# First head's maxima and shift made in the projection stage of an attention and expert kernel

## The chip, the cores and the metric

The kernel runs on one core of a Trainium2 chip. TensorE (PE) multiplies matrices; PEld is its weight load. VectorE (DVE), ScalarE (ACT) and GpSimd (POOL) work on tiles in SBUF and PSUM; SyncE (SP) issues most of the DMAs. Each engine takes its own instructions in the order in which they were written and waits at semaphores for the others. The metric is the device time of one execution in microseconds (us), the median of several runs.

## The reference, cut to what matters

```python
def reference(x, Wq, bq, Wk, bk, Wv, bv, Wo, bo, wg, bg, w1, b1, w2, b2, gamma, beta):
    xn = _layernorm(x)                      # x: 4 x 2048 x 256
    # attention, 16 heads of 16
    q, k, v = (heads(xn @ W.T + b) for W, b in ((Wq, bq), (Wk, bk), (Wv, bv)))
    probs = softmax(einsum('bqhd,bkhd->bhqk', q * 0.25, k))
    att = einsum('bhqk,bkhd->bqhd', probs, v).reshape(b, s, d) @ Wo.T + bo
    # experts: every token keeps 2 of 16, every expert takes 1024 of 2048 tokens of a batch
    scores = softmax(xn @ wg + bg)
    masked = scores * one_hot(top_k(scores, 2)).sum(-2)
    route = masked / (masked.sum(0) + 1e-6) * 4
    _, seq_ids = top_k(transpose(route), 1024)
    ...
    return x + att + layernorm(xn + scattered_expert_outputs) * gamma + beta
```

## The kernel before

Four stages run one after the other, each in a block of its own; at the end of a block all engines wait for each other.

- `norm`: layernorm of 16 blocks of 512 tokens, the transposed tokens into `tok_all`, v into `v_all`, the router's `logits`.
- `project`: q and k of all heads. A chunk is one half (128 features) of q or k for one block of 512 tokens: two matmuls into `qk_ps[m]` (L385), m = 0 to 3 over q's and k's halves, so 64 chunks. ACT takes each chunk out of PSUM twice: in full precision into `f32s[m]` (L409) and rounded into `parts[m]` (L411). POOL puts the rest that the rounding left beside it (L424), and SP stores both parts to `q_parts` and `k_parts` in DRAM (L432), 512 KB a chunk. PE may write `qk_ps[m]` again when ACT has rounded the chunk four before, and ACT may round when the store of the chunk four before has landed. So PE is at most eight chunks ahead of the stores that have landed. Beside this DVE makes the routing weights, a chain of small operations (L447 to L482). After a quarter of the blocks (16 chunks) PE waits for them (`routed`), transposes them into `route_ps` (L394), four PSUM banks, and DVE copies them to `route` (L484).
- `attend`: 64 heads (16 for each of 4 batches). A head's scores are computed twice. The first pass (`pass1`, L771) takes one part of 48 rows of `q_feat` and `k_feat` to `m_ps`, a piece of 128 queries by 1024 keys in two matmuls, 32 pieces a head; DVE takes the maximum of every piece (L852). From the maxima comes the head's `shift`: `row_max` (L854), rounded on ACT (L731), split on POOL (L579), turned on DVE (L843), put into two rows of `q_feat` by four DMAs (L653). The second pass (`score`, L781) uses the upper 50 rows with the shift in them; ACT takes exp (L724) and `weigh` (L790) multiplies with v. `q_feat` and `k_feat` have two buffers each, filled by `feed` (L641 to L647) with four DMAs: a pair of parts of q, k's first part twice, and one single part of each, 768 KB in all, once for the lower rows (first pass) and once for the upper ones (second pass). In the steady steps the first pass of the next heads runs between the scores of this one. Ahead of the first step all 32 pieces of head 0 and `EARLY` = 10 pieces of head 1 run alone (L820 to L825).
- `finish`: experts, output projection, final layernorm and sum.

The steps in SP's order at the start of `attend` are: feed head 0 and head 1 low, load two bias rows, feed head 0 up (after ACT has written ones into the last 32 rows of `k_feat`, L718), feed head 2 low, put the shift.

## Time and profile before

| | us |
|---|---|
| median of 3 runs | 3444.11 (3443.16 to 3446.69) |
| the profiled execution | 3444.21 |
| its span, first to last instruction | 3442.4 |
| `norm`, from the start to PE's first chunk | 102.2 |
| `project`, to the first instruction of `attend` on POOL | 102.2 to 239.2 |
| start of `attend`, to PE's first score of head 0 | 239.2 to 315.8 |
| from that score to the end | 315.8 to 3442.4 |

Over the whole span PE is busy for 96%, DVE for 84%, ACT for 73%, POOL for 27%. The stages differ much, so the busy shares have to be read by stage. In the rows further down a line like "150.38 3.60 PE L385 MATMUL ... x8" is a start, a duration in us, engine, line and operation, and the count of records; two chunks leave eight records, since each of their four matmuls leaves two. In square brackets stands the idle time before and what ended it.

### The profile page before, as it was taken

To read this page: it belongs to the slowest core of one execution; us is meant where nothing else is said; L and a number is where in the kernel's file an instruction comes from. 1 tells how busy PE (TensorE), PEld (TensorE's weight loads), DVE (VectorE), ACT (ScalarE), POOL (GpSimd) and SP (SyncE) were. 2 spreads that over 40 slices of the span, in tenths; PEclk is the share of its full clock that TensorE was granted. 3 is DMA by queue.
4 is the path that set the end of the run, shared out by engine and by line. 5 is a ranking of instruction groups with operands and counts; after the bars stand their busy time and mean duration, and the time that the engine had idled before them with its cause. 6 is when DMAs were issued, how large, how long until landed. Compare 5 with 4: busy or idle time off the path is not lost. (4 is left out here: it accounts for less than half of the span.)

```text
span 3442.4 us, 74610 instructions
## 1 busy us (share of the span) xinstructions
PE 3296.2 (96%) x20848; PEld 1706.4 (50%) x20848; DVE 2894.2 (84%) x2987; ACT 2526.4 (73%) x5726; POOL 929.1 (27%) x1339
## 2 busy tenths in 40 slices
PE   7868999999999999999999999999999999599998
PEld 6424444444444444444444444444444444288887
DVE  7508999999999999999999999999999998267777
ACT  3452888888888888888888888888888888443433
POOL 2550222222222222222222222222222222144443
PEclk9986999999999999999999999999999999799999
DMA  6581111122111211111121111211111121355553
GB/s 198 173 241 33 50 54 54 54 60 59 58 56 55 56 56 55 54 54 54 54 60 56 56 55 54 63 56 56 55 54 54 54 59 47 112 136 169 160 164 117
DMA packets 133063, 272.29 MB, mean 79 GB/s; under 512 B 22512, under 2 KB 68656, under 8 KB 120432
## 3 DMA queue, kind: packets, MB, share of 16 engines
q1 hardware_dynamic: 130464, 266.68, 26.7%
q8 instruction: 176, 2.88, 0.4%
q10 hardware_dynamic: 2256, 1.36, 0.2%
q14 instruction: 167, 1.37, 0.1%
HBM read 173.59 MB, written 84.93 MB: 75 GB/s over the span
## 5 line engine op out<-in xcount | busy, mean ns | idle before, releaser
L852 DVE TENSOR_REDUCE half_max<-m_ps 128x1 f32<-128x1024 f32 x2048 | 2413.4, 1220 | 324.5 <-PE m_ps L771 308.8
L724 ACT ACTIVATE prob<-s_ps 128x512 f32<-128x512 f32 (+1 forms) x5120 | 2188.3, 520 | 425.8 <-PE s_ps L781 423.2
L781 PE MATMUL s_ps<-q_feat,k_feat 50*128 50x512 f32 (+1 forms) x5120 | 1538.0, 396 | 7.5 <-issue 4.7
L771 PE MATMUL m_ps<-k_feat,q_feat 48*128 48x512 f32 x4096 | 1405.1, 448 | 55.9 <-DMA k_feat<-k_parts 28.4
L781 PEld LDWEIGHTS s_ps<-q_feat,k_feat 50*128 50x128 f32 x5120 | 796.2, 184 | 983.3 <-ACT prob L724 870.6
L790 PE MATMUL a_ps<-prob,v_head 128*32 128x512 f32 x8192 | 1091.6, 605 | 0.0
L771 PEld LDWEIGHTS m_ps<-k_feat,q_feat 48*128 48x128 f32 x4096 | 616.3, 187 | 287.5 <-DVE half_max L852 248.6
L579 POOL TENSOR_TENSOR shift<-row_max,shift 128x16 fp32r<-128x16 f32 x64 | 14.2, 222 | 1213.0 <-ACT shift L731 1213.0
L790 PEld LDWEIGHTS a_ps<-prob,v_head 128*32 128x32 f32 x8192 | 161.2, 108 | 253.7 <-issue 211.7
L1134 ACT ACTIVATE g_hi<-g 128x512 fp32r<-128x512 f32 x128 | 81.0, 632 | 243.8 <-DVE g L1172 199.8
L1297 POOL TENSOR_TENSOR g_lo<-g,g_hi 128x512 fp32r<-128x512 f32 x128 | 173.0, 1352 | 229.2 <-ACT g_hi L1134 229.2
L606 POOL TENSOR_SCALAR step_of<-route,cand 64x256 f32<-64x256 f32 x217 | 198.6, 915 | 44.5 <-POOL held L607 38.3
L573 POOL COPY v_head<-v_all 128x256 f32 (+1 forms) x64 | 25.3, 397 | 660.2 <-PE a_ps L790 660.1
L607 POOL TENSOR_TENSOR held<-held,step_of 64x256 f32<-64x256 f32 x217 | 157.6, 726 | 39.8 <-POOL step_of L606 39.8
L1172 DVE TENSOR_TENSOR g<-g,mask_bc 128x512 f32<-128x512 f32 x128 | 133.5, 1043 | 36.0 <-ACT g L1131 30.7
L1067 PE MATMUL o_ps<-w_hi,g_hi 128*128 128x256 f32 x512 | 144.6, 282 | 6.1 <-issue 3.7
L1067 PE MATMUL o_ps<-w_lo,g_hi 128*128 128x256 f32 x512 | 144.3, 282 | 0.0
L1067 PE MATMUL o_ps<-w_hi,g_lo 128*128 128x256 f32 x512 | 143.1, 280 | 0.0
L1056 PE MATMUL h_ps<-xn_hi,w_hi 128*128 128x512 f32 x256 | 105.7, 413 | 32.0 <-DMA b_rows<-b_parts 32.0
L1131 ACT ACTIVATE g<-h_ps,b_col 128x512 f32<-128x512 f32 x128 | 86.2, 674 | 25.7 <-PE h_ps L1056 25.7
L1067 PEld LDWEIGHTS o_ps<-w_hi,g_hi 128*128 128x128 f32 x512 | 96.5, 189 | 12.0 <-issue 7.1
L1056 PE MATMUL h_ps<-xn_lo,w_hi 128*128 128x512 f32 x256 | 102.1, 399 | 0.0
(132 smaller groups left out, 1904.1 us busy)
## 6 DMA issues: line engine op xcount, KB each, us to landing
q_feat<-q_parts SPq DMA_DIRECT2D x128, 256.0 KB
k_feat<-k_parts SPq DMA_DIRECT2D x128, 256.0 KB
q_parts<-parts SPq DMA_DIRECT2D x32, 512.0 KB, 4.8
k_parts<-parts SPq DMA_DIRECT2D x32, 512.0 KB, 4.8
q_feat<-q_parts SPq DMA_DIRECT2D x128, 128.0 KB
k_feat<-k_parts SPq DMA_DIRECT2D x128, 128.0 KB
att_dram<-att SPq DMA_DIRECT2D x64, 256.0 KB, 14.0
mask_bc<-mask_b SPq DMA_DIRECT2D x128, 128.0 KB, 4.4
```

The lines of the kernel that those rows point to most:

```text
L606: do(pool.tensor_scalar(step_of[:, :], t["route"][:, c * PART:(c + 1) * PART], bound, None, ALU.is_ge))
L607: do(pool.tensor_tensor(held[:, :], held[:, :], step_of[:, :], ALU.add))
L724: act.activation(prob[tile(r, kt) % R][:, cols(j)], s_ps[slot(r, kt, j) % R][:, wide(j)], ACT.Exp).then_inc(exped, 1)
L771: ins = pe.matmul(m_ps[p % 2][:, k * BLK:(k + 1) * BLK], q_feat[r % 2][LOW, qt * P:(qt + 1) * P], k_feat[r % 2][LOW, key:key + BLK], start ...
L781: pe.matmul(s_ps[slot(r, kt, j) % R][:, wide(j)], k_feat[r % 2][UP, kt * P:(kt + 1) * P], q_feat[r % 2][UP, cols(j)], start=True, stop=Tru ...
L790: ins = pe.matmul(a_ps[qb * VW:(qb + 1) * VW, :], v_head[r % R][:, kt, :], prob[tile(r, kt) % R][:, qb * BLK:(qb + 1) * BLK], start=(kt == ...
L852: dve.tensor_reduce(half_max[r][:, p // 2, p % 2:p % 2 + 1], m_ps[p % 2][:, :], AX.X, ALU.max).then_inc(maxed, 1)
L1056: ins = pe.matmul(h_ps[e % 2][:, :], w, v, start=(c == 0 and k == 0), stop=(c == KC - 1 and k == 2))
L1067: ins = pe.matmul(o_ps[k], v, w[:, e, :], start=(e == 0 and m == 0), stop=False)
L1131: act.activation(g[e % 2][:, :], h_ps[e % 2][:, :], ACT.Gelu, bias=b1_col[:, e:e + 1]).then_inc(gelu, 1)
L1172: dve.tensor_tensor(g[e % 2][:, :], g[e % 2][:, :], mask_bc[q % 2][:, e % QTR, :], ALU.mult).then_inc(gated, 1)
L1297: pool.tensor_tensor(g_lo[e % 2][:, :], g[e % 2][:, :], g_hi[e % 2][:, :].bitcast(F32), ALU.subtract).then_inc(split, 1)
```

## The change

The tiles `q_feat`, `k_feat`, `half_max`, `row_max`, `shift`, `turned` and the two `m_ps` buffers, with their semaphores, now live from the projection stage on. Room is made in SBUF by keeping the weights of v and the router in `norm`, by two buffers of `f32s` in place of four, and by doing the routing in `logits` and two `work` tiles instead of four. In PSUM the routing weights are transposed into `m_ps`.

In `project` PE runs six blocks (24 chunks) before it waits for the routing. The remaining 40 chunks are written out in 20 turns of two chunks and two or three pieces: 32 pieces of head 0 and 10 of head 1. DVE takes their maxima, and the shift of head 0 is made and put at the stage's end. SP issues three feeds between the stores. The ones in `k_feat` are written by POOL at the start of `norm`. `attend` starts with head 0's scores; SP feeds head 2 low first, then loads the biases.

```diff
@@ norm, gpsimd
             pool.sem_inc(rstd_done, 2)
+            pool.wait_ge(ident_made, 1)
+            for u in range(2):
+                pool.memset(t["k_feat"][u][96:P, :].bitcast(F32), 1.0).then_inc(cleared, 1)
+                pool.wait_ge(cleared, 3 + u)
@@ project
-    f32s = [sb(f"f32s{m}", [P, BLK]) for m in range(M)]
+    f32s = [sb(f"f32s{m}", [P, BLK]) for m in range(KC)]
...
-    work = sb("work", [P, 4, TILES, E])
-    ex, tmp, hot, hot2 = (work[:, k] for k in range(4))
+    work = sb("work", [P, 2, TILES, E])
+    ex, tmp = (work[:, k] for k in range(2))
+    hot, hot2 = lg[:, :, :], tmp
@@ project, tensor
-            chunks(0, NBLK // 4)
+            def first_pass(n, p):
+                if p == 0:
+                    pe.wait_ge(fed_low[n], 16 * LOADS)
+                pe.wait_ge(maxed, n * PAIRS + p + 1)
+                qt, half = divmod(p, 2)
+                for k in range(2):
+                    key = half * 2 * BLK + k * BLK
+                    ins = pe.matmul(m_ps[p % 2][:, k * BLK:(k + 1) * BLK], q_feat[n][low, qt * P:(qt + 1) * P],
+                                    k_feat[n][low, key:key + BLK], start=True, stop=True)
+                ins.then_inc(piece, 1)
+
+            with pe.Fori(0, BEFORE) as blk:
+                for m in range(M):
+                    chunk(blk, m)
 
             pe.wait_ge(routed, 1)
...
-            chunks(NBLK // 4, NBLK)
+            early = PAIRS + EARLY
+            turns = (NBLK - BEFORE) * M // 2
+            for blk in range(BEFORE, NBLK):
+                for m in range(M):
+                    chunk(blk, m)
+                    if m % 2 == 1:
+                        at = ((blk - BEFORE) * M + m) // 2
+                        for p in range(at * early // turns, (at + 1) * early // turns):
+                            first_pass(p // PAIRS, p % PAIRS)
@@ project, scalar
-                    act.wait_ge(split, blk * M + m + 1)
-                    act.activation(f32s[m][:, :], qk_ps[m][:, :], ACT.Identity, bias=biases[m][:, m % KC:m % KC + 1], scale=scales[m])
+                    act.wait_ge(split, blk * M + m + 1 + M - KC)
+                    act.activation(f32s[m % KC][:, :], qk_ps[m][:, :], ACT.Identity, bias=biases[m][:, m % KC:m % KC + 1], scale=scales[m])
...
+            act.wait_ge(row_maxed, 1)
+            act.activation(shift[:, 0, :], row_max[0][:, :], ACT.Copy).then_inc(shift_rounded, 1)
@@ project, gpsimd
+            pool.wait_ge(shift_rounded, 1)
+            pool.tensor_tensor(shift[:, 1, :], row_max[0][:, :], shift[:, 0, :].bitcast(F32), ALU.subtract).then_inc(shift_done, 1)
@@ project, sync
-            with sp.Fori(0, NBLK) as blk:
-                for m in range(M):
-                    sp.wait_ge(split, blk * M + m + 1 + M)
-                    store(blk, m)
+            stores(0, BPS + 1)
+            for m in range(M):
+                sp.wait_ge(stored[m], 16 * BPS + 16)
+            feed(0, LOWER, fed_low)
+            stores(BPS + 1, BPS + 3)
+            feed(1, LOWER, fed_low)
+            stores(BPS + 3, BPS + 5)
+            feed(0, UPPER, fed_up)
+            stores(BPS + 5, NBLK)
+            sp.wait_ge(shift_turned, 1)
+            rows = q_feat[0][UPPER + FEAT:UPPER + FEAT + SHIFT, :].bitcast(F32).rearrange("k (q j p) -> k q j p", j=quarters, q=ST)
+            for j in range(quarters):
+                sp.dma_start(rows[:, :, j, :], turned[j * SHIFT * ST:(j + 1) * SHIFT * ST, :]).then_inc(shift_in, 16)
@@ project, vector
-            do(dve.tensor_copy(t["route"][:, :], route_ps[:, :]))
+            for half in range(2):
+                do(dve.tensor_copy(t["route"][:, half * 2 * BLK:(half + 1) * 2 * BLK], m_ps[half][0:B * E, :]))
+            dve.sem_inc(maxed, 2)
+            for p in range(PAIRS):
+                dve.wait_ge(piece, p + 1)
+                dve.tensor_reduce(half_max[0][:, p // 2, p % 2:p % 2 + 1], m_ps[p % 2][:, :], AX.X, ALU.max).then_inc(maxed, 1)
+            dve.wait_ge(maxed, PAIRS + 2)
+            dve.tensor_reduce(row_max[0][:, :], half_max[0][:, :, :], AX.X, ALU.max, negate=True).then_inc(row_maxed, 1)
+            for p in range(EARLY):
...
+            dve.wait_ge(shift_done, 1)
+            dve.transpose(turned[:, :], shift[:, :, :].rearrange("p k q -> p (k q)").bitcast(F32)).then_inc(shift_turned, 1)
@@ attend, sync
-            for n in range(2):
-                feed(n, n, LOWER, fed_low)
+            sp.wait_ge(piece, PAIRS)
+            feed(2, 0, LOWER, fed_low)
             for dst, src in ((shift_bc[:, :], "beta"), (staged[:, 0:D].bitcast(F32), "bo")):
                 sp.dma_start(dst, t[src].partition_broadcast(P)).then_inc(bias_in, 16)
-            sp.wait_ge(ones_made, 2)
-            feed(0, 0, UPPER, fed_up)
-            sp.wait_ge(piece, PAIRS)
-            feed(2, 0, LOWER, fed_low)
-            put_shift(0, 0)
@@ attend, tensor
-            for p in range(PAIRS):
-                for k in range(2):
-                    pass1(0, 0, 0, p, k)
-            for p in range(EARLY):
-                for k in range(2):
-                    pass1(1, 0, 1, p, k)
             step(0, 0, 0, first=True)
```

On PE, from the end of `project` to the first score of head 0 (`s_ps`), this is the order before:

```order
L385 MATMUL qk_ps<-tok_all,wkT_sb 128x512 x2
L380 REGISTER_ALU
L380 COMPARE_AND_BRANCH
L376 UNCONDITIONAL_BRANCH
L757 UNCONDITIONAL_BRANCH
L771 MATMUL m_ps<-k_feat,q_feat 128x512 x84
L781 MATMUL s_ps<-q_feat,k_feat 128x512
```

and this after, from the last turns of `project` on (L411 is a chunk's matmul, L423 a piece's):

```order
L411 MATMUL qk_ps<-tok_all,wqT_sb 128x512 x4
L423 MATMUL m_ps<-k_feat,q_feat 128x512 x4
L411 MATMUL qk_ps<-tok_all,wkT_sb 128x512 x4
L423 MATMUL m_ps<-k_feat,q_feat 128x512 x6
L404 UNCONDITIONAL_BRANCH
L819 UNCONDITIONAL_BRANCH
L843 MATMUL s_ps<-q_feat,k_feat 128x512
```

All 84 matmuls of pieces have moved ahead of the block's end (L404); the first score stands right behind it.

On PE behind the wait for the routing, the order after (with what each waits for); the first piece waits for head 0's feed and stands ahead of all chunks but two:

```order
L434 MATMUL m_ps<-ident,work 64x128 [waits p_routed]
L434 MATMUL m_ps<-ident,work 64x128 x15
L411 MATMUL qk_ps<-tok_all,wqT_sb 128x512 [waits p_rounded]
L411 MATMUL qk_ps<-tok_all,wqT_sb 128x512
L411 MATMUL qk_ps<-tok_all,wqT_sb 128x512 [waits p_rounded]
L411 MATMUL qk_ps<-tok_all,wqT_sb 128x512
L423 MATMUL m_ps<-k_feat,q_feat 128x512 [waits a_maxed,a_fed_low0]
L423 MATMUL m_ps<-k_feat,q_feat 128x512
L423 MATMUL m_ps<-k_feat,q_feat 128x512 [waits a_maxed]
L423 MATMUL m_ps<-k_feat,q_feat 128x512
L411 MATMUL qk_ps<-tok_all,wkT_sb 128x512 [waits p_rounded]
```

Before, the chunks behind the transposes waited for `p_rounded` alone.

On SP, from the last store of the fifth block on, the order after:

```order
L485 DMA k_parts<-parts 128x2x512 [waits p_split]
L497 REGISTER_ALU
L497 COMPARE_AND_BRANCH
L491 DMA q_feat<-q_parts 32x1x2048 [waits p_stored2,p_stored3,p_stored1,p_stored0]
L492 DMA k_feat<-k_parts 32x1x2048
L493 DMA q_feat<-q_parts 16x2048
L494 DMA k_feat<-k_parts 16x2048
L497 UNCONDITIONAL_BRANCH
L497 ISA
L485 ISA [waits p_split]
L485 DMA q_parts<-parts 128x2x512
```

The stores of the blocks that follow now stand behind the feed in SP's queue; before, the same four DMAs (L644 to L647) stood behind the end of the block.

## Rows read from the trace of the kernel before

**Rows 1.** Windows by stage: busy time and count of each engine, clock share, DMA share, GB/s.

```profile
102.00:239.00 137.00, 115.02 (x272) 51.72 (x272) 40.27 (x33) 82.59 (x129) 88.60 (x66) 0.93 0.84 245
239.00:316.00 77.00, 49.54 (x86) 21.28 (x88) 50.16 (x44) 3.92 (x3) 5.28 (x9) 0.50 0.19 49
316.00:3442.00 3126.00, 3051.42 (x20108) 1568.33 (x20108) 2729.27 (x2637) 2405.35 (x5528) 814.22 (x1225) 0.99 0.24 69
```

**Rows 2.** Timeline of PE, end of `norm` to the end of `project`.

```profile
91.48 1.04 PE L320 MATMUL xT_ps<-ident,xn 128*128 128x128 f32 x8
102.20 3.69 PE L385 MATMUL qk_ps<-tok_all,wqT_sb 128*128 x8 [1.27 <-ACTq L401]
...
142.22 3.62 PE L394 MATMUL route_ps<-ident,work 128*64 128x128 f32 x16 [12.29 <-DVE cand L482]
145.63 4.91 PE L385 MATMUL qk_ps<-tok_all,wqT_sb 128*128 x8
150.38 3.60 PE L385 MATMUL qk_ps<-tok_all,wkT_sb 128*128 x8
153.82 3.60 PE L385 MATMUL qk_ps<-tok_all,wqT_sb 128*128 x8
...
225.92 3.60 PE L385 MATMUL qk_ps<-tok_all,wkT_sb 128*128 x8
```

**Rows 3.** Timeline of PE, DVE, ACT and POOL, start of `attend`.

```profile
239.24 1.80 POOL L566 MEMSET prob<- 32x2048 f32 x1 [4.29 <-POOLq L376]
257.87 2.07 PE L771 MATMUL m_ps<-k_feat,q_feat 48*128 48x512 f32 x4 [28.35 <-DMA k_feat<-k_parts]
262.94 2.35 PE L771 MATMUL m_ps<-k_feat,q_feat 48*128 48x512 f32 x4 [0.18 <-DVE half_max L852]
264.19 2.36 DVE L852 TENSOR_REDUCE half_max<-m_ps 128x1 f32<-128x1024 f32 x2 [0.17 <-PE m_ps L771]
315.78 0.76 PE L781 MATMUL s_ps<-q_feat,k_feat 50*128 50x512 f32 x1 [4.75 <-issue]
```

**Rows 4.** Timeline of SP: pairs of stores, then the first DMA of a feed.

```profile
108.38 2.41 SPq L432 DMA_DIRECT2D q_parts<-parts  x2
134.72 2.58 SPq L432 DMA_DIRECT2D k_parts<-parts  x2
232.20 3.15 SPq L432 DMA_DIRECT2D k_parts<-parts  x2
298.25 0.65 SPq L644 DMA_DIRECT2D q_feat<-q_parts  x1
```

**Rows 5.** Windows of one us behind the feed issued at 298.25, columns as in rows 1.

```profile
303.00:304.00 1.00, 0.91 (x3) 0.47 (x2) 1.00 (x2) 0.00 (x0) 0.00 (x0) 0.50 0.14 57
310.00:311.00 1.00, 1.00 (x2) 0.32 (x2) 1.00 (x1) 0.00 (x0) 0.00 (x0) 0.50 0.14 57
312.00:313.00 1.00, 0.00 (x0) 0.00 (x0) 0.30 (x1) 0.00 (x0) 0.00 (x0) 0.50 0.83 131
```

**Rows 6.** Windows in `project`, columns as in rows 1.

```profile
180.00:230.00 50.00, 49.52 (x116) 21.66 (x114) 0.00 (x0) 36.06 (x57) 36.15 (x29) 1.00 0.99 295
```

**Rows 7.** Timeline: POOL in `norm`, splits on POOL, a routing operation on DVE, PE in a steady step.

```profile
8.35 0.22 POOL L287 TENSOR_SCALAR var<-mv 128x4 f32<-128x4 f32 x1 [6.77 <-DVE mv L230]
121.45 15.45 POOL L424 TENSOR_TENSOR parts<-f32s,parts 128x512 fp32r<-128x512 f32 x8 [0.26 <-ACT parts L411]
153.65 1.27 POOL L424 TENSOR_TENSOR parts<-f32s,parts 128x512 fp32r<-128x512 f32 x1 [0.45 <-ACT parts L411]
135.81 1.37 DVE L474 TENSOR_TENSOR denom<-work 128x256 f32<-128x256 f32 x1
346.52 1.06 PE L790 MATMUL a_ps<-prob,v_head 128*32 128x512 f32 x8
347.51 0.38 PE L781 MATMUL s_ps<-q_feat,k_feat 50*128 50x256 f32 x1
349.07 1.06 PE L790 MATMUL a_ps<-prob,v_head 128*32 128x512 f32 x8
```

More of the change, by code:

```diff
@@ L58 @@
 PART = 256
+HEAD_RING = 3
+PAIRS = ST * 2
+EARLY = 10
+LOADS = 4
+BEFORE = 6
 HALVES = NBLK * KC
@@ L133, in build @@
             cand = sb("cand", [B * E, 1], I32, ctx=first)
+            q_feat = [sb(f"q_feat{r}", [P, S], F32R, ctx=first) for r in range(2)]
+            k_feat = [sb(f"k_feat{r}", [P, S], F32R, ctx=first) for r in range(2)]
+            half_max = [sb(f"half_max{r}", [P, ST, 2], ctx=first) for r in range(HEAD_RING)]
+            row_max = [sb(f"row_max{r}", [P, ST], ctx=first) for r in range(HEAD_RING)]
+            shift = sb("shift", [P, SHIFT, ST], F32R, ctx=first)
+            turned = sb("turned", [P, SHIFT * ST], ctx=first)
+            fed_low = [sem(f"a_fed_low{r}") for r in range(2)]
+            fed_up = [sem(f"a_fed_up{r}") for r in range(2)]
+            piece, maxed, row_maxed = sem("a_piece"), sem("a_maxed"), sem("a_row_maxed")
+            shift_rounded, shift_done = sem("a_shift_rounded"), sem("a_shift")
+            shift_turned, shift_in = sem("a_shift_turned"), sem("a_shift_in")
             mid = ExitStack()
@@ L146, in build @@
                     norm(nc, sem, lambda *a: sb(*a, ctx=st), lambda *a: ps(*a, ctx=st), locals())
+                banks = first.enter_context(ExitStack())
+                m_ps = [ps(f"m_ps{r}", [P, 2 * BLK], banks) for r in range(2)]
                 with ExitStack() as st:
@@ L378, in _ @@
         def _(pe):
-            def chunks(lo, hi):
-                with pe.Fori(lo, hi) as blk:
-                    for m in range(M):
-                        pe.wait_ge(rounded, blk * M + m + 1)
-                        for c in range(KC):
-                            half = m % KC
-                            ins = pe.matmul(qk_ps[m][:, :], weights[m][:, c, half * P:(half + 1) * P],
-                                            t["tok_all"][:, ds(blk, 1), c * BLK:(c + 1) * BLK].rearrange("p n s -> p (n s)"),
-                                            start=(c == 0), stop=(c == KC - 1))
-                        ins.then_inc(scored, 1)
@@ L390, in _, with chunk @@
-            chunks(0, NBLK // 4)
+            def chunk(blk, m):
+                pe.wait_ge(rounded, blk * M + m + 1)
+                for c in range(KC):
+                    half = m % KC
+                    ins = pe.matmul(qk_ps[m][:, :], weights[m][:, c, half * P:(half + 1) * P],
+                                    t["tok_all"][:, ds(blk, 1), c * BLK:(c + 1) * BLK].rearrange("p n s -> p (n s)"),
+                                    start=(c == 0), stop=(c == KC - 1))
+                ins.then_inc(scored, 1)
@@ L499, in attend @@
     QUARTERS = P // (SHIFT * ST)
-    LOADS = 4
     ROUNDS = (HEADS - 4) // U
     SHIFT_LOADS = QUARTERS
-    q_feat = [sb(f"q_feat{r}", [P, S], F32R) for r in range(2)]
-    k_feat = [sb(f"k_feat{r}", [P, S], F32R) for r in range(2)]
+    q_feat, k_feat, half_max, row_max, shift, turned = (t[w] for w in ("q_feat", "k_feat", "half_max", "row_max", "shift", "turned"))
     prob = [sb(f"prob{r}", [P, S]) for r in range(R)]
@@ L508, in attend @@
     att = sb("att", [P, BLK])
-    half_max = [sb(f"half_max{r}", [P, ST, 2]) for r in range(R)]
-    row_max = [sb(f"row_max{r}", [P, ST]) for r in range(R)]
-    shift = sb("shift", [P, SHIFT, ST], F32R)
-    turned = sb("turned", [P, SHIFT * ST])
     s_ps = [ps(f"s_ps{r}", [P, BLK]) for r in range(R)]
-    m_ps = [ps(f"m_ps{r}", [P, 2 * BLK]) for r in range(2)]
+    m_ps = t["m_ps"]
     a_ps = ps("a_ps", [P, BLK])
@@ L715, in _ @@
             act.sem_inc(att_read, 1)
-            act.wait_ge(ones_set, 1)
-            for u in range(2):
-                act.activation(k_feat[u][96:P, :], prob[0][96:P, :], ACT.Copy).then_inc(ones_made, 1)
             def exp(g, r, kt, j):
```

78 lines of the change are left out of this document (42 added, 36 removed).

## The prediction

> **What bounds the kernel now.** I read the windows by stage first, then PE's timeline in the two stages that the change touches, then SP's queue and the DMA share there. The windows [rows 1] show three stretches. From 316 us on PE is busy for 3051 of 3126 us at a clock share of 0.99: whatever the change does ahead of that, this part is bounded by PE and keeps its length if it starts in the same state. In `project`, 137 us long, PE is busy for 115 us and the DMA engines have a share of 0.84. The 77 us behind it are the poor ones: the clock share is 0.50, which is 1.2 GHz, DMA 0.19, ACT and POOL nearly idle.
>
> In `project` PE starts at 102.20 and puts out two chunks every 3.43 us (150.38 to 153.82), so 1.717 us a chunk [rows 2]. It stood still once, 12.29 us for the routing, and came back at 1.2 GHz: its 16 transposes took 3.62 us where 8 took 1.04 at 2.4 GHz, and the first pair of chunks took 4.91 [rows 2]. Its last matmul ends at 229.5. The block ends at 239.2 [rows 3], 9.7 us later: rounding, split, store and landing of the last chunks. From 154 on the DMAs have no room either: in 180 to 230 us their share is 0.99 at 295 GB/s [rows 6], with PE never idle. A store of 0.524 MB at that rate takes 1.78 us, a hair more than PE's 1.72. PE bounds this stretch, and DMA stands right behind it.
>
> In the start of `attend` nothing can run before the first feed: PE's first piece starts at 257.87 after 28.35 us of idle [rows 3]. The pieces then go at DVE's pace: two reduces take 2.36 us and come every 2.53, and PE waits 0.18 us for DVE each time [rows 3]. 42 pieces are 53 us. Then PE waits 4.75 us for the shift's DMAs, and the first score starts at 315.78 [rows 3], 76.5 us after the block's start.
>
> **What goes.** All of that stretch but the way from the block's start to the first score, which in the changed kernel waits only for DMAs that are issued ahead of the block's end. I take 1 us for it. So 75.5 us go, and what `project` grows by comes back.
>
> **What PE gets in `project`.** The 84 matmuls of pieces. In a steady step the time from one `weigh` to the next is 2.55 us (346.52 to 349.07), of which `weigh` takes 0.99 (to 347.51) [rows 7]; the other 1.56 us hold 4096 columns, eight matmuls' worth, so 0.20 us for one of 512 columns at 2.4 GHz. 84 of them are 16.8 us; six stand behind the last chunk and fall beside its store, so 15.6 count. DVE's reduces (1.2 us a piece, 2.6 a turn of 4.3) are hidden in a turn with two pieces; in the one inner turn with three PE waits about 1 us, since the third needs the first one's buffer.
>
> **The routing's wait.** 24 chunks take 41.2 us, to 143.4; before, the weights were ready at 142.2 [rows 2]. The chain will be slower now, since POOL keeps splitting beside it: eight splits beside the routing took 15.45 us and one alone 1.27, and a small DVE operation beside them took 1.37 [rows 7]. I take 145, with bounds of 142 (no effect) and 148. PE waits 1.6 us in place of 12.3, and stays at 2.4 GHz, so the transposes take 2.1. Doing the routing in two tiles changes no operation's size: nothing. Halving `f32s` makes ACT wait for the split two chunks before: at 1.27 us against 1.72 a chunk it costs nothing from 145 on; ahead of that the split's 1.93 paces ACT as it did before, and PE's four PSUM buffers cover it. The memsets of ones (1.80 us each [rows 3]) lie in POOL's idle 6.77 us at the start of `norm` [rows 7]: nothing; 3.6 us less idle there is left over.
>
> **The feeds.** This is the term that decides. The feed issued at 298.25 [rows 4] ran alone. Behind a short burst the DMA share was 0.14 at 57 GB/s from 303 to 311, and the next burst came at 312 [rows 5]. So a feed holds a few engines for 11 to 13 us, while the other engines idle; a share of 0.14 of 16 engines is two. The two pairs are 512 KB of its 768, and 57 GB/s for 9 us is just that. [...] If instead the 0.79 MB went over all engines at the 295 GB/s of rows 6, a feed would be 2.7 us and the sum near that of the first rival below.
>
> The stores' share of 0.99 [rows 6] shows them on all 16 engines, so three feeds put some 33 us on the two that every store passes. It costs PE in two places.
>
> First, the wait for head 0's feed. It is issued behind the stores of block 4. The last store of block 3 was issued at about 137 (134.72 and 2.58 for the pair), the first at 108.4 [rows 4]: 1.88 us a store, so four more come to 144.5. Alone it would land 13.5 us later (298.25 to 312); about 1.5 stores queued ahead make 161. PE gets to the first piece at 145 + 2.1 + 3.4 = 150.5 and waits 10.5 us; bounds 3 (the pairs find room at once) and 17. Behind such a wait the clock is at 1.2 GHz: the transposes and the pair of chunks behind the old wait took 8.2 us for 5.5 us of work, so 2.6 us more. Before, the routing's wait cost the same.
>
> Second, the other two feeds hold back the stores. PE can be eight chunks ahead of the landed ones. From the end of the first feed (159) the two engines do 16 stores (20 to 35) at 1.75 and two feeds of 11, to 209; store 36 lands at 211, and with its rounding PE can start chunk 44 at 213. Unhindered it would get there at 203 to 204 (18 chunks of 2.14 us with their pieces, from 164). So 9 us; bounds 0 (the feeds find gaps) and 21 (15 us a feed).
>
> **The sum.** PE's last chunk ends at 102.2 + 109.9 (64 chunks) + 2.1 + 15.6 + 1.6 (routing) + 10.5 + 2.6 + 1 + 9 = 254.5. The DMA side gives the same: from 211 on 27 stores of 1.75 are 258 and a landing. For the rest of the block, 9.7 us before, I take 9: the four DMAs of the shift are issued while the last stores land. The block ends at 263.5, the first score starts at 264.5, before it was 315.8: 51.3 us less. In the first step nothing is late: head 2's low feed, now first in SP's queue, is due at the eleventh key tile, 28 us in; the upper feed of head 1, behind it, is due 41 us in, and lands by 25 with the biases between. PE enters the step at 1.2 GHz as it did [rows 1]. The profiled execution was 3444.2 us (0.1 above the median), so 3393.
>
> **Rivals.** (1) The feeds cost the stores nothing, since the two engines have gaps that the share of 0.99 hides, and the first lands quickly. Then PE alone sets the end: 16.5 us of the terms above go (the 9, and 7.5 of the first wait), the first score comes near 248, the time is 3376. For it: PE, not DMA, paced the stores in rows 6, and the pieces stretch a turn of two stores from 3.43 to 4.3 us. Against it: 11 us on two engines is more than that room for ten stores.
>
> (2) The feeds cost more: beside stores each needs 15 us, since a packet of one waits for packets of the other. Then the first wait grows by 4 and the second by 8: 3405.
>
> (3) Slower. PE does not come back to 2.4 GHz behind the wait for the feed. In rows 1 it stayed at 0.50 for the whole 77 us, though it was busy for 49.5 of them, with the same small matmuls. 40 chunks and 84 matmuls at half the clock are 68.7 + 16.8 us more, less the 2.6 counted: 3476, 32 slower than before. It turns into a loss if PE stays low for over 0.6 of those turns. Against it: after the routing's wait PE was back in 6 us [rows 2], and a turn is four fifths the same chunks.
>
> (4) The change doesn't do what it says: the first score is held at the block's start for a shift or a feed that lands late, and some 10 us are given back (3403). The upper feed of head 0 is issued behind block 8, 60 us earlier, and the shift takes four small DMAs; little speaks for it.
>
> **How the numbers follow.** The forecast, 3393 with 3385 to 3400 around it for the routing and the first wait, has a chance of 0.55; rival 1 0.22, rival 2 0.15, rival 4 0.05, rival 3 0.03. The range takes in rivals 1, 2 and 4: 3374 to 3407. A measurement of this kernel can tell some 0.2% (7 us) from no change. All cases but rival 3 are faster by more: faster 0.96, same 0.01, slower 0.03.
>
> **What would show it.** In the changed profile: PE idle for 1 to 4 us for the routing in place of 12; PE idle some 10 us near 150 for a DMA into `k_feat` or `q_feat` (3 for rival 1, over 14 for rival 2); ACT waiting for landings of stores around 185 to 210, with PE short of chunks; granted clock 1.00 from 170 on (0.50: rival 3); `attend` starting between 256 and 270 with its first score about 1 us later, and 3126 us from there to the end. I am wrong if the time from the first score to the end has changed by over 5 us, or if the pieces make a turn longer than 4.6 us with no wait for DMA in it.

## The result and the profile after

The changed kernel takes 3486.16 us (median of 4 runs, 3485.2 to 3488.71), the kernel before in the same session 3444.88; the ratio is 1.012, with a 95% interval of 1.0107 to 1.0132. It is 41 us slower, where 51 us less was forecast. The profiled execution has a span of 3483.5 us.

What the forecast said of the projection stage came close. Timeline of PE, end of `norm` to the first score, answering to [rows 2] and [rows 3] (start us, us, engine, line, operation, output<-inputs, shape, count, idle time ahead and what ended it):

```profile
145.68 1.94 PE L434 MATMUL m_ps<-ident,work 128*64 128x128 f32 x16 [2.09 <-DVE cand L558]
147.45 3.60 PE L411 MATMUL qk_ps<-tok_all,wqT_sb 128*128 128x512 f32 x8
159.77 2.07 PE L423 MATMUL m_ps<-k_feat,q_feat 48*128 48x512 f32 x4 [8.71 <-DMA k_feat<-k_parts]
161.77 5.30 PE L411 MATMUL qk_ps<-tok_all,wkT_sb 128*128 128x512 f32 x8
...
186.03 1.19 PE L423 MATMUL m_ps<-k_feat,q_feat 48*128 48x512 f32 x4
188.46 5.40 PE L411 MATMUL qk_ps<-tok_all,wqT_sb 128*128 128x512 f32 x8 [1.25 <-ACT parts L460]
193.79 1.19 PE L423 MATMUL m_ps<-k_feat,q_feat 48*128 48x512 f32 x4
194.91 3.70 PE L411 MATMUL qk_ps<-tok_all,wkT_sb 128*128 128x512 f32 x8
198.54 1.20 PE L423 MATMUL m_ps<-k_feat,q_feat 48*128 48x512 f32 x4
199.67 3.70 PE L411 MATMUL qk_ps<-tok_all,wqT_sb 128*128 128x512 f32 x8
...
210.10 0.73 PE L423 MATMUL m_ps<-k_feat,q_feat 48*128 48x512 f32 x2 [0.85 <-DVE half_max L565]
212.44 5.40 PE L411 MATMUL qk_ps<-tok_all,wqT_sb 128*128 128x512 f32 x8 [1.61 <-ACT parts L460]
...
256.91 3.70 PE L411 MATMUL qk_ps<-tok_all,wkT_sb 128*128 128x512 f32 x8
...
269.09 0.76 PE L843 MATMUL s_ps<-q_feat,k_feat 50*128 50x512 f32 x1 [5.77 <-ACTq L780]
```

PE waits 2.09 us for the routing and 8.71 us for head 0's feed, is held twice by stores that land late, ends its last chunk at 260.6 and starts the first score at 269.09; before it was 315.78 [rows 3]. So 46.7 of the 51.3 us are gained by then.

The loss is behind that point, in the part whose length the forecast held fixed. From the first score to the end it is 3483.5 - 269.1 = 3214.4 us, and before 3442.4 - 315.8 = 3126.6: 87.8 us more. The lists of ACT's waits (us in total, times, longest) differ in one line, of which the first row is the kernel before and the second the changed one. ACT's timeline of the changed kernel shows one of the nine waits:

```profile
ACT prob L724 <- issue: 1.2, 5, 0.3
...
ACT prob L787 <- issue: 49.6, 9, 5.8
...
600.55 0.66 ACT L787 ACTIVATE prob<-s_ps 128x256 f32<-128x256 f32 x2 [0.42 <-PE s_ps L843]
606.98 2.14 ACT L787 ACTIVATE prob<-s_ps 128x512 f32<-128x512 f32 x5 [5.78 <-issue]
```

The 5.78 us lie between the last exponential of the sixth head in ACT's loop and the first of the next round, at the loop's jump back (the branch from the end of the loop's code to its start). The loop has ten rounds of six heads and so nine jumps back, and each has its wait, of 5.15 to 5.78 us. "Issue" means that ACT waited for nothing that the profile shows. PE stands behind it, and its clock falls. PE's first matmul after the wait, and windows around it (busy us and count of PE, PEld, DVE, ACT and POOL, then granted clock, DMA share, GB/s):

```profile
607.63 0.58 PE L843 MATMUL s_ps<-q_feat,k_feat 50*128 50x256 f32 x1 [4.88 <-ACT prob L787]
...
604.00:608.00 4.00, 0.37 (x2) 0.37 (x2) 0.00 (x0) 1.02 (x3) 0.00 (x0) 0.67 0.15 55
608.00:612.00 4.00, 4.00 (x17) 1.39 (x15) 2.36 (x2) 2.75 (x7) 0.00 (x0) 0.50 0.13 51
612.00:616.00 4.00, 4.00 (x29) 2.24 (x26) 2.78 (x3) 3.39 (x9) 3.08 (x5) 0.98 0.08 31
```

From one rounding of a head's shift to the next (ACT, L794) a steady head takes 41.15 us, the nine heads with such a wait 47.5 to 49.7; over the 61 heads from the third rounding to the last the sum is 2587.4 us, before 2518.7. That is 68.7 of the 87.8.

Most of the rest is the last head. In ACT's and PE's timelines and in the windows:

```profile
2951.35 2.82 ACT L787 ACTIVATE prob<-s_ps 128x512 f32<-128x512 f32 x6 [1.77 <-PE s_ps L843]
2952.00 1.05 PE L843 MATMUL s_ps<-q_feat,k_feat 50*128 50x512 f32 x3 [1.43 <-ACT prob L787]
...
2940.00:2960.00 20.00, 17.85 (x83) 7.13 (x81) 7.88 (x4) 14.65 (x34) 5.69 (x3) 0.84 0.22 68
2960.00:2980.00 20.00, 20.00 (x66) 7.15 (x65) 0.00 (x0) 11.22 (x26) 0.00 (x0) 0.50 0.00 1
2980.00:3000.00 20.00, 20.00 (x68) 6.96 (x71) 0.00 (x0) 11.26 (x25) 0.00 (x0) 0.50 0.00 0
```

PE stops once, for 1.4 us, and goes on at a granted clock of 0.50 to the head's end: a key tile (the scores and the `weigh` of 128 keys) takes 4.07 us there (2962.93 to 2966.99 between ACT's exponentials) in place of 2.55. From one collection of a head (ACT copies its result out of PSUM, L799) to the next ( 2944.90, 3002.53) the last one takes 57.6 us, before 38.2 (L736: 2923.19, 2961.34): 19.4 us.

### The profile page after: what moved, and what is told of

It reads as the page before. It is cut to its first block and busy times, and to the rows that moved or that the text cites. A ratio compares the mean times of both kernels' runs of the same rounds, so it can differ in the third digit from the quotient of the medians.

```text
span 3483.5 us, 74499 instructions
## 1 busy us (share of the span) xinstructions
PE 3327.7 (96%) x20848; PEld 1716.1 (49%) x20848; DVE 2898.1 (83%) x2988; ACT 2528.3 (73%) x5724; POOL 933.4 (27%) x1340
## 3 DMA queue, kind: packets, MB, share of 16 engines
q10 hardware_dynamic: 2256, 1.36, 0.2%
q14 instruction: 166, 1.36, 0.1%
## 5 line engine op out<-in xcount | busy, mean ns | idle before, releaser
L906 DVE TENSOR_REDUCE half_max<-m_ps 128x1 f32<-128x1024 f32 x2006 | 2363.4, 1220 | 279.7 <-PE m_ps L833 264.2
L843 PE MATMUL s_ps<-q_feat,k_feat 50*128 50x512 f32 (+1 forms) x5120 | 1560.2, 402 | 50.0 <-ACT prob L787 43.3
L833 PE MATMUL m_ps<-k_feat,q_feat 48*128 48x512 f32 x4012 | 1367.9, 446 | 23.6 <-DVE half_max L906 23.4
L843 PEld LDWEIGHTS s_ps<-q_feat,k_feat 50*128 50x128 f32 x5120 | 810.6, 188 | 1044.5 <-ACT prob L787 916.4
L852 PE MATMUL a_ps<-prob,v_head 128*32 128x512 f32 x8192 | 1114.3, 617 | 0.3 <-ACT prob L787 0.3
L833 PEld LDWEIGHTS m_ps<-k_feat,q_feat 48*128 48x128 f32 x4012 | 605.4, 187 | 225.0 <-DVE half_max L906 215.4
L475 POOL TENSOR_TENSOR parts<-f32s,parts 128x512 fp32r<-128x512 f32 x64 | 89.1, 1400 | 72.5 <-ACT parts L460 71.9
```

The source lines that it names most:

```text
L475: pool.tensor_tensor(parts[m][:, 1, :], f32s[m % KC][:, :], parts[m][:, 0, :].bitcast(F32), ALU.subtract).then_inc(split, 1)
L833: ins = pe.matmul(m_ps[p % 2][:, k * BLK:(k + 1) * BLK], q_feat[r % 2][LOW, qt * P:(qt + 1) * P], k_feat[r % 2][LOW, key:key + BLK], start ...
L843: pe.matmul(s_ps[slot(r, kt, j) % R][:, wide(j)], k_feat[r % 2][UP, kt * P:(kt + 1) * P], q_feat[r % 2][UP, cols(j)], start=True, stop=Tru ...
L852: ins = pe.matmul(a_ps[qb * VW:(qb + 1) * VW, :], v_head[r % R][:, kt, :], prob[tile(r, kt) % R][:, qb * BLK:(qb + 1) * BLK], start=(kt == ...
L906: dve.tensor_reduce(half_max[r][:, p // 2, p % 2:p % 2 + 1], m_ps[p % 2][:, :], AX.X, ALU.max).then_inc(maxed, 1)
```

## The experiments

**What ACT's program looks like.** The change takes four instructions out of what ACT runs ahead of its loop over the heads (the ones rows are no longer copied by ACT, which is three, its loop in `project` is two shorter, and one for the shift is added). In the compiled program 272 instructions of ACT stand ahead of the loop's hint (`hint_back_edge=True`) before, 268 in the changed kernel. The loop itself is the same, 1083 instructions. Theory A: the waits are ACT's wait for its own code, and a shift by four places decides. The rivals: TensorE's code (62 instructions longer ahead of its loop), the feeds, or the new places of tiles in SBUF and PSUM. "Place" is, below, the number of ACT's instructions ahead of the hint.

**Four instructions put back.** Edit in the changed kernel, in `attend` on ACT (`placed` is a semaphore that nobody reads):

```diff
             act.sem_inc(exped, R)
             act.sem_inc(att_read, 1)
+            for _ in range(4):
+                act.sem_inc(placed, 1)
```

> The changed kernel, with four increments of an unused semaphore put in front of ScalarE's first wait in the attention, so that ScalarE's loop over the heads begins and ends four instructions later, on the same count (272 instructions ahead of it) as in the kernel before; no other engine's code moves and nothing is computed otherwise. Theory A (the 87.8 us lost after the first score come from where ScalarE's loop lies in its instruction memory: at each jump back it waits 5.2 to 5.8 us for its code): the nine waits of ScalarE at the loop's end go, the heads there take 41.15 us again instead of 47.5 to 49.7, which is 68 us; the median is 3486 - 68 = 3418, and 3398 if the low clock of the last head (another 20 us) hangs on it too. Rival B (the feeds or the code of TensorE, 62 instructions longer ahead of its loop, are what holds ScalarE): stays at 3486. Rival C (the tiles that are now allocated for the whole of the first stages lie elsewhere in SBUF and PSUM and cost port or bank conflicts): stays at 3486.

Measured: 3398.66 us (3398.25 to 3399.3), ratio to the kernel before 0.9858 (0.9842 to 0.9875). The nine waits are gone and the last head is at a granted clock of 1.00. Timeline of ACT at the first jump back, then one window over the last head, of this run:

```profile
602.22 0.66 ACT L790 ACTIVATE prob<-s_ps 128x256 f32<-128x256 f32 x2 [0.42 <-PE s_ps L846]
603.15 3.74 ACT L790 ACTIVATE prob<-s_ps 128x512 f32<-128x512 f32 x8 [0.27 <-issue]
...
2879.00:2919.00 40.00, 37.22 (x208) 13.86 (x208) 4.09 (x2) 32.48 (x76) 2.01 (x2) 1.00 0.11 34
```

The first score starts at 270.52, and from there to the end (3396.5) it is 3126.0 us, the kernel before's 3126.6 within a microsecond. All 87.8 us hung on the four instructions, those of the last head too. No other engine's code moved in this run.

**The same place in the kernel before.** The opposite edit, with the serial start of the attention left as it was:

```diff
@@ attend, gpsimd
-            pool.memset(prob[0][96:P, :], 1.0).then_inc(ones_set, 1)
-            pool.wait_ge(ones_set, 1)
+            for u in range(2):
+                pool.memset(k_feat[u][96:P, :].bitcast(F32), 1.0).then_inc(ones_made, 1)
+            pool.wait_ge(ones_made, 2)
...
@@ attend, scalar
-            act.sem_inc(exped, R)
-            act.sem_inc(att_read, 1)
-            act.wait_ge(ones_set, 1)
-            for u in range(2):
-                act.activation(k_feat[u][96:P, :], prob[0][96:P, :], ACT.Copy).then_inc(ones_made, 1)
@@ attend, vector
+            dve.sem_inc(att_read, 1)
+            dve.sem_inc(exped, R)
```

> The kernel before, with ScalarE's loop over the heads four instructions earlier (268 ahead of it, as in the changed kernel): the ones rows are written by two memsets of GpSimd instead of two activations of ScalarE, and two initial increments are given by VectorE. Order of work, feeds and serial start of the attention stay as before. Theory A (the placement of ScalarE's loop alone): the jumps back now cost 5 us each, nine heads lengthen by 6 to 8 us and the time is 3445 + 68 = 3513, up to 3533 if the last head runs at the low clock too. Rivals B and C (TensorE's code, the feeds, the tiles' places): stays at 3445 within 3.

Measured: 3511.43 us (3507.94 to 3520.12), ratio 1.0182 (1.0165 to 1.0199), 64 us slower. Its list of waits has the line again:

```profile
ACT prob L720 <- issue: 48.9, 9, 5.8
```

Its last head stayed at a granted clock of 1.00 (windows from 2980 to 3022 us), which is why it lost 64 us and not 88. The rivals fall: in this run TensorE's code, the feeds and the tiles are those of before. What is shown, by both directions, is that the place of ACT's code makes the waits; that they are waits for code is argued in the next part.

**Is it the loop's code?** The profile lists queues of kind "instruction" apart from those that move data. In the changed kernel's page they are these (packets, MB, share of 16 engines):

```profile
q8 instruction: 177, 2.90, 0.4%
q14 instruction: 166, 1.36, 0.1%
```

A packet has 16 KB on the one (2.90 MB in 177) and 8 KB on the other (1.36 MB in 166). That they bring the engines' code is taken from the name of the kind. The stretch of the wait in the changed kernel, 601.2 to 604.5 and 604.5 to 605.0, and then the last 2 us ahead of the jump in the run with four increments (601.0 to 603.1), each with what its queues moved:

```profile
q1 hardware_dynamic: 185, 0.53, 73.8%
q8 instruction: 1, 0.02, 3.4%
```

```profile
q1 hardware_dynamic: 4, 0.02, 13.4%
q14 instruction: 1, 0.01, 5.2%
```

```profile
q1 hardware_dynamic: 16, 0.13, 22.8%
q14 instruction: 2, 0.02, 3.0%
```

```profile
ACT prob L790 <- issue: 58.4, 9, 6.7
```

This is one run, and the hint is an instruction itself: the loop starts where it would at place 271 with a hint, between the good 270 and 272. A hint that does nothing would have left the time at 3399. At the good place the hint is worth nine waits of up to 6.7 us, 72 us in all. If 58.4 us is what the waits come to without a hint anywhere, then at 268 the hint saves 9 us of it, and at 266 nothing (below: 58.4 us, longest 6.9); no run takes the hint away at a bad place. How the hint does it the runs don't show: the 8 KB queue moves two packets in the last 2 us ahead of the first jump without it as with it (599.0 to 601.1 here, 601.0 to 603.1 above), and still ACT waits 6.47 us there, with one packet more 4.6 us into the wait. It is the same at the other eight jumps, where that packet comes 4.4 to 4.9 us into the wait.

**Which places?** Thirteen more places, one run each; the kernel before took 3444.6 to 3448.5 us in these sessions, so differences of under 5 us between rows say nothing. For 269 and 270 the edit is the one above with 1 and 2 increments, for 266 the two initial increments go to DVE, and for the rest the increments stand at the end of ACT's work in `project`, where it is idle.

> The changed kernel with two such increments instead of four (270 instructions ahead of ScalarE's loop). Theory A with a sharp edge between two positions in a block of code: either as the changed kernel (3486, nine waits of 5 us) or as with four (3418 or below, none), and which of the two says on which side of 270 the edge lies. If the wait grew smoothly with the distance, it would be near half, 3452 or so. Rivals B and C: 3486.

> The changed kernel with one increment in front of ScalarE's first wait in the attention (269 instructions ahead of its loop; 268 had nine waits of 5.2 to 5.8 us at the loop's end, 270 had none in the loop but a stop and the low clock in the last head, 272 neither). Theory A1 (a sharp edge in the place of the loop's first instruction, between 268 and 270): either all nine waits, 3475 to 3490, or none of them, 3420 to 3427. Theory A2 (the wait shrinks with the distance, and 270 is where it has gone): some 2 to 3 us a wait, 3450 or so.

> The changed kernel with ScalarE's loop two instructions earlier (266 ahead of it): the two initial increments are given by VectorE. So far 268, 396 and 524 had the nine waits, 269, 270 and 272 had none. Theory E (from 269 on there is a range without the wait, below it there is one with it): nine waits, 3475 to 3490. Theory F (places that are bad lie singly, at 268 and every 128 or fewer instructions from it): none at 266, 3420 to 3427.

> The changed kernel with 8 increments at the end of ScalarE's work in the projection stage (276 ahead of its loop). Theory E (a range without the wait from 269 on): none, 3399 to 3425. Theory F with a period of 8: the nine waits, 3475 to 3490.

> The same with 24 increments (292 ahead of the loop): theory E with a range of 24 or more: no waits, 3399 to 3425; if the range ends before, or if the good places are the narrow ones: nine waits, 3475 to 3490. The pair with 276 says which.

> The same with 64 increments (332 ahead of the loop). Theory E with a wide range (the place counts by blocks, half of which are good): no waits, 3399 to 3425. If the good range is a narrow one, or the bad places come every 64: nine waits, 3475 to 3490.

> The changed kernel with 96 increments at that place (364 ahead of the loop). Where does the good range end? Theory G with a bad range of a few places below each edge: none, 3425 to 3440 (the stop in the last head comes 14 key tiles earlier than with none, so more of it at the low clock). Theory H (a bad range of half of the 128 or more): nine waits.

> The changed kernel with 112 increments at that place (380 ahead of the loop). Theory G with a bad range under 16 places: no waits, 3425 to 3440; with a bad range of 16 or more: nine waits, 3475 to 3500.

> The changed kernel with 128 increments at the end of ScalarE's work in the projection stage (396 instructions ahead of its loop), where ScalarE is idle for over 10 us. Theory A (what matters is how the loop's ends lie in blocks of 256 instructions): half a block from the bad place no wait at the jumps back, the heads take 41.15 us, about 3399 to 3425, the upper end if a stop in the last head puts TensorE at the low clock. Theory D (ScalarE's whole code is too long for its memory, and more code ahead of the loop can only make it worse): 3486 or more.

> The changed kernel with 129 increments at the end of ScalarE's work in the projection stage (397 instructions ahead of its loop). So far 266, 268, 396 and 524 have the nine waits, 269, 270, 272, 276, 292 and 332 have none. Theory G (the places repeat every 128 instructions, with the same edge as between 268 and 269): no waits, near 3425 with the stop in the last head at the place that one increment gives. Rival (one wide good range of 269 to somewhere short of 396 in each block of 256): nine waits, about 3484.

> The changed kernel with 192 increments at that place (460 ahead of the loop, between the bad 397 and 524). Theory K with one good and one bad range in each 256: nine waits, 3485 to 3500. If there is a further good range in it: none, 3405 to 3435.

> The changed kernel with 256 increments at the same place (524 instructions ahead of ScalarE's loop, one block of 256 more than the changed kernel's 268). Theory A with a period of 256 instructions: the nine waits of 5 us are back, 3475 to 3490. If the period is another one, or only the distance from the start of the program counts: none, 3399 to 3425.

> The changed kernel with 260 increments at the end of ScalarE's work in the projection stage (528 instructions ahead of its loop, 256 more than the good 272). Theory K (the place counts modulo 256): no waits at the jumps back, and the first score 12 us later than without increments, as with 256 of them: 3408 to 3415. Rival (no period of 256; from 396 on all places are bad): nine waits, near 3500.

| place (increments) | us | nine waits at the jump back, sum and longest | last heads at clock 0.50 |
|---|---|---|---|
| 266 (-2) | 3469.5 | 58.4, 6.9 | no |
| 268 (0) | 3486.2 | 49.6, 5.8 | yes |
| 269 (1) | 3425.5 | none | yes |
| 270 (2) | 3424.4 | none | yes |
| 272 (4) | 3398.7 | none | no |
| 276 (8) | 3396.9 | none | no |
| 292 (24) | 3426.4 | none | yes |
| 332 (64) | 3432.9 | none | yes |
| 364 (96) | 3405.3 | none | no |
| 380 (112) | 3407.4 | none | no |
| 396 (128) | 3483.5 | 48.7, 5.7 | yes |
| 397 (129) | 3490.2 | 49.6, 5.8 | yes |
| 460 (192) | 3442.2 | none | yes |
| 524 (256) | 3501.4 | 49.8, 5.8 | yes |
| 528 (260) | 3499.2 | 48.4, 5.8 | yes |

(192, 256 and 260 increments also hold the first exponential back: PE waits 12.8, 17.6 and 17.8 us for its first score in place of 5.8.)

The edge at 268 is sharp: one instruction is worth 61 us. Four rules of the expectations fell: blocks of 256, a length that the author assumed, with a good place half a block from a bad one (396 is bad), singly placed bad spots below 268 (266 has them), a period of exactly 128 (397 has them, 269 has not), a period of 256 with one good half (460 is good, 528 bad). What is left is a description. All six bad places lie 10 to 16 above a multiple of 128 (266, 268, 396, 397, 524, 528), and the six that lie 20 to 124 above one (276, 292, 332, 364, 380, 460) are all good; in the first group 269, 270 and 272 are good, so the edge is not in the same place above each multiple: 13 above is good at 269 and bad at 397, 16 above good at 272 and bad at 528. Why, the runs don't say.

**The last heads** have a rule of their own. There the code is straight, and the stop moves with the code. With 24 and 64 increments it is at 2877.8 and 2861.7 us (both ahead of the last head), 16 us or 6.3 key tiles earlier for 40 more instructions, and a key tile is 6 to 7 of ACT's instructions. With 128 it is where it was with none (6.0 and 6.5 us behind the collection of the head before). The profile does not name "issue" here: it puts ACT's gap down to PE, and PE's to ACT (below, and 2951.35 and 2952.00 above), so that ACT's code is behind it is argued from this movement. The place alone does not decide what it costs: in the kernel before with its loop at 268, ACT's gap there is 0.72 us (3002.02) and PE stays at a granted clock of 1.00. This is ACT's timeline in the run with 2 increments, its stop in the last head, then a window of that run, and under it the same window of the run with 4:

```profile
2890.61 2.14 ACT L790 ACTIVATE prob<-s_ps 128x512 f32<-128x512 f32 x5 [2.09 <-PE a_ps L855]
...
2900.00:2920.00 20.00, 20.00 (x65) 7.09 (x65) 0.00 (x0) 11.55 (x25) 0.00 (x0) 0.50 0.00 1
```

```profile
2900.00:2920.00 20.00, 17.43 (x104) 6.32 (x96) 0.00 (x0) 14.57 (x35) 0.00 (x0) 1.00 0.01 5
```

With 96 increments ACT's stop is longer, 2.75 us, but pieces of the first pass still follow it, and PE is back by the window of 2870 (granted clock 1.00). With 112 it is 4.62 us, and PE comes back too (1.00 from 2866 on). Behind the stops at 2861.7 or later there are no pieces or hardly any (two matmuls with 64 increments); PE is then busy for 20 of 20 us at a clock of 0.50 and does not come back before the end of the attention. So the same kind of stop costs about 7 us in one place (3405.3 against 3398.7; by the trace 5.4, 46.18 against 40.74 between the last two roundings of a shift), 19 in another, and 34 with 64 increments (3432.9), where nearly two heads run at 0.50. That the missing pieces are the reason is argued; no run changes them alone.

**The feeds.** The next two runs stand on the good place (272). The first is compared with 3398.7. In `project`, each transfer of two parts is cut in two (PE's waits for the added transfers are left out here):

```diff
-                pair, single = slice(where, where + 2 * HD), slice(where + 2 * HD, where + FEAT)
-                sp.dma_start(q_feat[n][pair, :].bitcast(F32), q).then_inc(done[n], 16)
-                sp.dma_start(k_feat[n][pair, :].bitcast(F32), k[0:1].broadcast_to([2, HD, S])).then_inc(done[n], 16)
+                single = slice(where + 2 * HD, where + FEAT)
+                for j, to in ((0, done[n]), (1, apart)):
+                    rows = slice(where + j * HD, where + (j + 1) * HD)
+                    sp.dma_start(q_feat[n][rows, :].bitcast(F32), q[j:j + 1].rearrange("k d s -> (k d) s")).then_inc(to, 16)
+                    sp.dma_start(k_feat[n][rows, :].bitcast(F32), k[0:1].rearrange("k d s -> (k d) s")).then_inc(to, 16)
```

> The changed kernel with the four increments, and the feeds of the projection stage cut into single parts: each of the two transfers of 32 rows (two parts) becomes two of 16 rows, six transfers a feed instead of four, with the same bytes. Theory: the transfers of two parts run on two DMA engines only (share 0.12 to 0.14, 57 GB/s in the rows), and so hold the first piece 8.7 us and the stores, and through them ScalarE's rounding and the chunks, another 6.4 us; cut into parts of 16 rows they spread over all engines, the first piece waits under 2 us and the two holes of 5.40 us shrink to the steady 3.70, which makes it 10 to 15 us faster than the run with the four increments alone (3403 to 3408 against 3418). Rival: the feeds are bound by something else (the rows' order, the queue), and it stays within 2 us of that run.

Measured: 3386.01 us (3385.0 to 3387.07), ratio to the kernel before 0.9822 (0.9805 to 0.9838): 12.7 us less than with the four increments alone, with the same bytes. PE's waits in the projection stage of this run, and its window from 102 to 239 us (its first score starts at 256.20):

```profile
PE m_ps L426 <- DMA k_feat<-k_parts: 2.5, 1, 2.5
...
102.00:239.00 137.00, 131.18 (x330) 57.92 (x329) 85.95 (x71) 77.21 (x121) 82.91 (x59) 0.99 0.86 239
```

The run with four increments alone has 7.0 us of that wait, a DMA share of 0.75 and 216 GB/s in the same window; of its stops of PE for ACT's rounding (3.3 us) 0.3 is left. Late in PE's wait for the feed the DMA share is 1.04 at 382 GB/s with the single parts, some of it stores (152 to 154 us), and 0.12 at 49 GB/s with the pairs of the changed kernel (156 to 158). So the shape of the pairs' transfers, not their bytes, made the wait and the stops. This is also the fastest kernel of the study, 1.8% below the kernel before and 2.9% below the changed one (0.9822 against 1.012).

**The pieces' price.** On top of the single parts, one piece behind each chunk in place of two behind every second:

```diff
-            turns = (NBLK - BEFORE) * M // 2
+            turns = (NBLK - BEFORE) * M
...
-                    if m % 2 == 1:
-                        at = ((blk - BEFORE) * M + m) // 2
-                        for p in range(at * early // turns, (at + 1) * early // turns):
-                            first_pass(p // PAIRS, p % PAIRS)
+                    at = (blk - BEFORE) * M + m
+                    for p in range(at * early // turns, (at + 1) * early // turns):
+                        first_pass(p // PAIRS, p % PAIRS)
```

> The run with the parts' feeds (3386.0), with the pieces one behind each chunk of the projection, in place of two behind every second chunk: the same chunks and the same 42 pieces, but the row of chunks is broken twice as often. A turn with two pieces took 4.755 us where two chunks alone take 3.43, so a piece's matmul costs 0.33 us in place of the 0.20 of the prediction. Theory S (of the 1.32 us, 1.12 is the four matmuls and 0.21 the change from chunks to pieces and back): the turn grows to 4.96 us, 3390 in all. Theory T (the price is per matmul, however they stand): the turn stays at 4.75, and the one wait of 0.85 us for a third piece goes: 3385.

Measured: 3394.22 us (3392.73 to 3395.89), 8.2 more than 3386.01. Timeline of PE in this run:

```profile
172.55 0.73 PE L426 MATMUL m_ps<-k_feat,q_feat 48*128 48x512 f32 x2
173.21 1.99 PE L413 MATMUL qk_ps<-tok_all,wkT_sb 128*128 128x512 f32 x4
175.12 0.73 PE L426 MATMUL m_ps<-k_feat,q_feat 48*128 48x512 f32 x2
175.78 1.98 PE L413 MATMUL qk_ps<-tok_all,wqT_sb 128*128 128x512 f32 x4
177.70 0.73 PE L426 MATMUL m_ps<-k_feat,q_feat 48*128 48x512 f32 x2
```

Two chunks with two pieces take 5.15 us (172.55 to 177.70) when each piece stands alone and 4.755 together (194.91 to 199.67 in the changed kernel), against 3.43 for the chunks alone [rows 2]. Four matmuls and two changes are 1.72, four and one are 1.32: so a change from chunks to pieces and back costs 0.40 us, and a matmul 0.23. Theory S was right, but a change costs twice what it said; 20 more changes are 8 us. That the time grew by 8.2 is partly luck: both waits of 0.85 us for a third piece went, and the first pieces came later and at the lower clock (PE waits 3.6 us for the feed in place of 2.5, and the transposes take 2.87 us in place of 1.94). The price stands on the rows of the steady turns.

## Why the prediction was wrong

The forecast was 3393 us, within 3374 to 3407, and slower had a chance of 0.03. The time is 3486.

**The step that failed** is the first one: "From 316 us on PE is busy for 3051 of 3126 us at a clock share of 0.99: whatever the change does ahead of that, this part is bounded by PE and keeps its length if it starts in the same state." It looked at PE, DMA and the feeds as what could carry over. What carried over was the place of ACT's code. The prediction named the test for itself ("wrong if the time from the first score to the end has changed by over 5 us"), and it changed by 87.8, but no rival had a mechanism for it. None of the four rivals is what happened: after head 0's feed PE was back at a granted clock of 1.00 (166 to 180 us, a pair of chunks in 3.63 us from 168.12 on), against the third. But that one's price for a low clock is the kind of thing that made a 1.4 us stop into 19 us. With the four instructions back the kernel takes 3398.7 us, 6 from the forecast and inside its range. The rest of the sum held, with some luck: the pieces cost 10 us more than said, and the feed, the stores and the block's end some 6 less.

**Its terms**, for the changed kernel:

- Serial start of the attention: 75.5 us expected to go. It went; the way from PE's last chunk to the first score is 8.5 us (260.6 to 269.1) where 10 was said.
- Routing: 1.6 us of wait expected, 2.09 measured; transposes 2.1, measured 1.8 (145.68 to 147.45).
- Pieces: 15.6 us expected at 0.20 a matmul. A turn grew by 1.32 us for four of them, so 19 turns make 25, and the third piece of the one long turn 0.7 more. This is the term that was mis-sized, by 10 us: the price was taken from a place in the steady attention where small matmuls follow small ones, and the 0.40 us of each change was missing (8 of the 10 us; the rest is 0.23 against 0.20 a matmul). By the prediction's own mark (a turn over 4.6 us with no wait in it) it was wrong here.
- Head 0's feed: 10.5 us of wait expected, 8.71 measured; clock recovery behind it 2.6 expected. The pieces took 2.00 in place of 1.12 and the chunks 5.23 in place of 3.63, which is 2.5.
- Three pieces in a turn: 1 us expected, 0.85 measured.
- Stores held back by the feeds: 9 us expected. Two stops of 1.25 and 1.61 us for ACT's rounding, with a slow pair of chunks behind each (5.40 in place of 3.70), are 6.3.

They add up to 101.8 + 109.9 + 2.1 + 1.8 + 26 + 8.7 + 2.5 + 0.9 + 6.3 = 260, and PE's last chunk ended at 260.6, six later than forecast. The first rival (feeds cost nothing) has the mechanism of the run with single parts, though that needed another edit, and with the pieces' 10 us its first score at 248 becomes 258, against 256.2 there. In that run the same bytes in transfers of 16 rows made PE wait 2.5 us in place of 7.0.

## What to carry to other kernels

ACT's loop has 1083 instructions here, and an edit far ahead of it cost a wait of 5.15 to 5.78 us at each of its nine jumps back. After an edit ahead of such a loop look in the list of waits for an engine's wait for "issue" that occurs once a round, and if it is there, move the loop by a few instructions before judging the edit. Price an operation that is put between others by a row where it stands between such others, not among its own kind (a piece's matmul cost 0.33 us in the turns, 0.20 by the row of the prediction). Look at the length of every stretch that "cannot change", since a forecast that is right to 6 us on its own terms was wrong by 88 on the one it took as given.

## What the runs showed of the hardware that was not expected

- One instruction more or less ahead of ACT's loop (268 against 269) was worth 61 us of 3486: nine waits of 5.15 to 5.78 us, the first of them followed by some 4 us of PE at a granted clock of 0.50 (608 to 612).
- The loop's hint is worth 72 us at a good place (3470.6 us without it, 3398.7 with it) and, by the waits, nearly nothing at a bad one (nine waits of 5.5 us on average, against 6.5 in the run without the hint).
- The page of the changed kernel has two instruction queues, with packets of 16 KB (q8, 177 of them) and of 8 KB (q14, 166). The bad places found are 266 and 268, 396 and 397, 524 and 528, so about 128 instructions apart.
- Behind a stop of 1.4 us PE ran at a granted clock of 0.50 for the last 50 us of the attention, fully busy, while behind one of 2.64 us a head earlier (2852.48 in the run with 96 increments), with pieces of the first pass following, it was back at 1.00 in under 20 (the window of 2870).
- Breaking a row of matmuls of 128 rows with ones of 48 rows costs 0.40 us a time (two chunks and two pieces take 5.15 us with the pieces apart, 4.755 with them together).
